# Attention on Trainium2: batches outside and head pairs inside, values of two pairs at once, a split output product

## The reference

```
def _L0_xattn_ref(x, context, w_q, w_k, w_v, w_o, b_o):   # 16 heads of 64, SCALE = 64 ** -0.5
    q = (x @ w_q).reshape(B, Sq, HEADS, DIM_HEAD).transpose(0, 2, 1, 3)
    k = (context @ w_k).reshape(B, Skv, HEADS, DIM_HEAD).transpose(0, 2, 1, 3)
    v = (context @ w_v).reshape(B, Skv, HEADS, DIM_HEAD).transpose(0, 2, 1, 3)
    sim = jnp.einsum('bhid,bhjd->bhij', q, k) * SCALE
    attn = jax.nn.softmax(sim, axis=-1)
    out = jnp.einsum('bhij,bhjd->bhid', attn, v)
    out = out.transpose(0, 2, 1, 3).reshape(B, Sq, INNER)
    return out @ w_o + b_o
...
x = x + _L0_xattn_ref(_layernorm(x, axis=-1), ctx_768, ...)
x = x + _L0_ffn_ref(_layernorm(x, axis=-1), ...)
x = x + _L1_xattn_ref(_layernorm(x, axis=-1), ctx_768, ...)
x = x + _L1_ffn_ref(_layernorm(x, axis=-1), ...)
```

## Time and profile before

| | |
|---|---|
| median of 3 runs | 2856.79 us (2854.0 to 2858.03) |
| the profiled execution: its time, its span | 2852.76 us, 2851.0 us |
| TensorE, VectorE | 2647.2 us (93%), 1999.4 us (70%) |
| ScalarE, GpSimd | 1290.9 us (45%), 1336.2 us (47%) |
| attention phases | some 38 to 993 us, and one as long in the second layer |

### The profile page before, as it was taken

One profiled execution on the slowest core, in us unless ns is written; L12 is line 12 of the kernel. 1 busy time (PEld: TensorE's weight loads), 2 busy tenths in 40 slices (PEclk: granted clock), 3 DMA queues, 4 the chain that ended last, 5 costly groups with the idle time before them and its releaser, 6 DMA issues. The chain is left out here.

```text
span 2851.0 us, 40294 instructions
## 1 busy us (share of the span) xinstructions
PE 2647.2 (93%) x13254; PEld 1814.1 (64%) x13254; DVE 1999.4 (70%) x2552; ACT 1290.9 (45%) x1891; POOL 1336.2 (47%) x1054
## 2 busy tenths in 40 slices
PE   3999999999999879999999689999999999996895
PEld 2556565656565468888888555656565656554785
DVE  5677677777676567777777657677777767764795
ACT  3545454545454333333333344545454545443394
POOL 4665656565656501111111145656666565652245
PEclk9999999999999989999999789999999999997997
DMA  3111111111111020000000010111111101103312
GB/s 109 39 30 33 30 29 33 37 26 35 35 24 33 16 67 22 24 26 22 22 28 17 10 39 23 41 29 33 29 36 27 40 22 38 27 23 116 121 50 86
DMA packets 48850, 108.85 MB, mean 38 GB/s; under 512 B 7200, under 2 KB 22432, under 8 KB 47776
## 3 DMA queue, kind: packets, MB, share of 16 engines
q1 hardware_dynamic: 43952, 101.01, 12.5%
q0 software_dynamic: 1536, 4.20, 0.5%
q10 hardware_dynamic: 3312, 3.02, 0.3%
HBM read 47.64 MB, written 10.22 MB: 20 GB/s over the span
## 5 line engine op out<-in xcount | busy, mean ns | idle before, releaser
L372 POOL TENSOR_TENSOR L1a_psums<-L1a_psums,L1a_probs 128x512 f32<-128x512 f32 x384 | 481.3, 1302 | 50.0 <-ACT L1a_probs L407 50.0
L372 POOL TENSOR_TENSOR L0a_psums<-L0a_psums,L0a_probs 128x512 f32<-128x512 f32 x384 | 481.1, 1297 | 49.7 <-ACT L0a_probs L407 49.7
L471 DVE TENSOR_REDUCE L1a_row_max<-psum 128x2 f32<-128x2048 f32 x128 | 293.5, 2293 | 150.9 <-PE psum L584 150.8
L471 DVE TENSOR_REDUCE L0a_row_max<-psum 128x2 f32<-128x2048 f32 x128 | 293.5, 2293 | 150.7 <-PE psum L584 150.7
L802 POOL TENSOR_TENSOR L0e_w_lo<-L0e_raw,L0e_w_hi 128x768 fp32r<-128x768 f32 x34 | 63.7, 1873 | 497.7 <-ACT L0e_w_hi L816 497.7
L407 ACT ACTIVATE L1a_probs<-psum 128x1024 f32<-128x1024 f32 x256 | 253.4, 1025 | 76.7 <-PE psum L611 75.2
L407 ACT ACTIVATE L0a_probs<-psum 128x1024 f32<-128x1024 f32 x256 | 253.3, 1025 | 73.8 <-PE psum L611 72.2
L624 PE MATMUL psum<-L0a_probs,L0a_v 128*64 128x512 f32 x1024 | 247.3, 605 | 0.0
L624 PE MATMUL psum<-L1a_probs,L1a_v 128*64 128x512 f32 x1024 | 247.3, 604 | 0.0
L856 DVE SCALAR_TENSOR_TENSOR xres<-psum,L0e_weights_of,xres 128x256 f32<-128x256 f32 x544 | 225.6, 477 | 22.7 <-PE psum L1029 21.8
L372 POOL TENSOR_TENSOR L1a_psums<-L1a_probs 128x512 f32<-128x512 f32 x64 | 81.4, 1294 | 322.1 <-ACT L1a_probs L407 322.1
(11 more groups left out here) (348 smaller groups left out, 6224.4 us busy)
## 6 DMA issues: line engine op xcount, KB each, us to landing
L0a_k_hs<-L0a_k_st SPq DMA_DIRECT2D x64, 256.0 KB, 3.5
L1a_k_hs<-L1a_k_st SPq DMA_DIRECT2D x64, 256.0 KB, 3.4
L0e_raw<-in_experts SPq DMA_DIRECT2D x34, 384.0 KB, 3.0
L1weights<-in_sorted SPq DMA_DIRECT2D x2, 6144.0 KB, 17.9
L0a_q_hh<-L0a_q_hh SPq DMA_DIRECT2D x64, 128.0 KB, 2.3
L1a_q_hh<-L1a_q_hh SPq DMA_DIRECT2D x64, 128.0 KB, 2.3
L0a_raw<-in_attention SPq DMA_DIRECT2D x8, 384.0 KB, 3.2
L1a_raw<-in_attention SPq DMA_DIRECT2D x8, 384.0 KB, 3.1
```

The costliest lines, as they stand in the source:

```text
L372: nc.gpsimd.tensor_tensor(psums[:, h, :], a, probs[:, h, kv, :], ALU.add).then_inc(sem["acc"], 1)
L471: nc.vector.reduce_max(row_max[:, qt, 0:2 * 32].rearrange("p (h n) -> p h n", h=2)[:, :, 0], psum[:, 0:4 * BANK].rearrange("p (h k) -> p h ...
```

## The change

- Batches are the outer loop and head pairs the inner one. The context is loaded and split one batch ahead, in the first segment of each batch (`prepares`), and the first normalisation does only batch 0.
- Each segment has its own weights: loaded and split in each segment, into two alternating halves of `w_split`. ScalarE takes the high part, GpSimd (before: VectorE) the remainder. The output weights are part of them.
- Values are projected for two pairs at once, five products of 256 columns for each 128 keys, in one block ahead of the rounds in each even segment. One ScalarE copy replaces a copy and an addition.
- The rounds are two value products, then scores.
- The output is split: a copy on ScalarE (`high_output`), a subtraction on VectorE (`low_output`), and three fast products for each slow one.
- The high part of the queries is taken by VectorE (`high_queries`), the copies of keys on ScalarE follow the first exponentials, and VectorE's reciprocal stands ahead of K0's remainder. The bias is added by VectorE.

```
-WCOL = (KD + 4) * P
+WCOL = (KD + 2) * P + DIM
+VCOL = 4 * P
...
                     def run(eng, segment):
-                        segment(0, 0, first=True)
-                        with eng.Fori(0, HP - 1) as hp:
-                            for b in range(1, BATCH + 1):
-                                segment(hp, b)
-                        for b in range(1, BATCH):
-                            segment(HP - 1, b, ahead=b < BATCH - 1)
+                        for b in range(BATCH):
+                            segment((0, HP * b), b, first=b == 0)
+                            with eng.Fori(0, HP // 2 - 1) as r:
+                                segment((r, HP * b + 1), b)
+                                segment((r, HP * b + 2), b)
+                            segment((0, HP * b + HP - 1), b, ahead=b < BATCH - 1)
...
+                        def low_weights(s):
+                            par = s[1] % 2
+                            pool.wait_ge(sem["whi"], count(s, 1, 1))
+                            nc.gpsimd.tensor_tensor(w_split[:, par, 1, :], raw[:, :], w_split[:, par, 0, :], ALU.subtract)\
+                                .then_inc(sem["wlo"], 1)
...
+                        def high_output(s):
+                            act.wait_ge(sem["norm"], count(s, 1, 1))
+                            nc.scalar.activation(o_split[:, 0, :], o_sb[:, :], ACT.Copy).then_inc(sem["ohi"], 1)
+
+                        def segment(s, b, first=False, ahead=True):
+                            max_rows(s)
+                            exps(s, 0)
+                            exps(s, 1)
+                            if ahead:
+                                high_keys("K0", after(s))
+                            exps(s, 2)
+                            if ahead:
+                                high_keys("K1", after(s))
+                            exps(s, 3)
+                            exps(s, 4)
+                            if not first:
+                                high_output(before(s))
...
+                        def high_queries(s):
+                            par, src = s[1] % 2, bank(PLACE["Q"])
+                            dve.wait_ge(sem["proj"], count(s, 3, 3))
+                            for h in range(2):
+                                nc.vector.tensor_copy(q_hh[HEAD[h], par, h, :], src[HEAD[h], :]).then_inc(sem["qhi"], 1)
...
+                        def low_output(s):
+                            dve.wait_ge(sem["ohi"], count(s, 1, 1))
+                            nc.vector.tensor_tensor(o_split[:, 1, :], o_sb[:, :], o_split[:, 0, :], ALU.subtract).then_inc(sem["olo"], 1)
...
-                        def project_values(piece, hp, b, added=True):
-                            batch, n = b % BATCH, VALUES.index(piece)
...
-                                nc.tensor.matmul(both, ctx_hi[:, keys_of], w_split[:, :, WV[0]], start=True, stop=False)
-                                nc.tensor.matmul(both, ctx_hl[:, keys_of], w_split[:, :, WV[1]], start=False, stop=False)
-                                last = nc.tensor.matmul(both[:, 0, :], ctx_lo[:, keys_of], w_hi[:, WV[0]], start=False, stop=True)
...
+                                last = split_product(bank(PLACE[piece])[:, i * 2 * P:(i + 1) * 2 * P],
+                                                     [(hi, wv[:, 0, WV[0]]), (hi, wv[:, 1, WV[0]]), (lo, wv[:, 0, WV[0]]),
+                                                      (hl, wv[:, 0, WV[1]]), (hl, wv[:, 1, WV[1]])])
...
-                                pe.wait_ge(sem["norm"], count(hp, 1, b, 1))
-                                pe.wait_ge(sem["wo"], (hp + b // BATCH) * 16 + 16)
+                                pe.wait_ge(sem["olo"], count(s, 1, 1))
...
-                                last = nc.tensor.matmul(bank(PLACE[f"OUT{half}"])[:, n * DIM:(n + 1) * DIM],
-                                                        o_sb[:, t * P:(t + 1) * P], wo_sb[:, :], start=True, stop=True)
+                                last = split_product(bank(PLACE[f"OUT{half}"])[:, n * DIM:(n + 1) * DIM],
+                                                     [(o_hi[:, rows], w_hi), (o_hi[:, rows], w_lo), (o_lo[:, rows], w_hi)])
...
+                            if even(s):
+                                for piece in VALUES:
+                                    project_values(piece, s, b, first)
                             for qt in range(QT):
-                                pv(hp, b, 2 * qt, first)
-                                pv(hp, b, 2 * qt + 1, first)
+                                pv(s, 2 * qt, first)
+                                pv(s, 2 * qt + 1, first)
                                 if ahead:
-                                    score(hp, b + 1, qt)
-                                    project_values(VALUES[qt], hp, b + 1, not first)
+                                    score(after(s), qt)
```

More of the change, by code:

```diff
@@ new lines, in segment @@
+                            for p in range(5, 8):
+                                exps(s, p)
+                            if even(s):
+                                for piece in VALUES:
+                                    values(piece, s)
+                            if s[1] != LAST[1]:
+                                if not first:
+                                    act.wait_ge(sem["out"], count(before(s), 2, 2))
+                                high_weights((s[0], s[1] + 3))
+                                if even(s):
+                                    high_values((s[0], s[1] + 2))
@@ L486, in add_output, with segment @@
                                 rows = xres[:, t:t + 2, :].rearrange("p t d -> p (t d)")
-                                dve.wait_ge(sem["out"], count(hp, 2, b, half + 1))
-                                dve.wait_ge(sem["added"], count(hp, 2, b, half + 3))
+                                dve.wait_ge(sem["out"], count(s, 2, half + 1))
+                                dve.wait_ge(sem["added"], count(before(s), 2, BEFORE + half + 1))
                                 nc.vector.tensor_tensor(rows, bank(PLACE[f"OUT{half}"]), rows, ALU.add).then_inc(sem["added"], 1)
-                        def segment(hp, b, first=False, ahead=True):
-                            split = b == BATCH - 2 and not isinstance(hp, int)
+                        def segment(s, b, first=False, ahead=True):
+                            if not first:
+                                invert(before(s))
@@ L526, in _ @@
+                        normalise(LAST)
+                        low_output(LAST)
+                        add_output(LAST, BATCH - 1)
                     @block.tensor
@@ L651, in output, with segment @@
                             last.then_inc(sem["out"], 1)
-                        def segment(hp, b, first=False, ahead=True):
+                        def segment(s, b, first=False, ahead=True):
+                            nb = (s[1] + 1) // HP if isinstance(s[0], int) else b
                             if ahead:
-                                keys("K0", hp, b + 1)
-                            transpose_max(hp, b, first)
+                                keys("K0", after(s), nb)
+                            transpose_max(s)
@@ L673, in segment @@
-                            qk(hp, b, 6)
-                            qk(hp, b, 7)
+                                output(before(s), 0, ahead)
+                            qk(s, 6)
+                            if not first and even(s):
+                                output(before(s), 1, ahead)
+                            qk(s, 7)
+                            if not first and not even(s):
+                                output(before(s), 1, ahead)
+                            if even(s):
+                                for piece in VALUES:
+                                    project_values(piece, s, b, first)
```

515 lines of the change are left out of this document (267 added, 248 removed).

## The result

The changed kernel takes 3270.9 us (median of 4, 3266.2 to 3274.6), beside 2855.4 for the kernel before in the same rounds: a ratio of 1.145, with an interval of 1.143 to 1.147. The direction and nearly all steps of the forecast of 3170 us came true; some 100 us came on top, and they have one cause.

The account below looks back on a forecast made before the run. TensorE, busy 93%, was taken to bound the kernel, VectorE's reduction close behind. Rounds −0.5, value block +2.4 and output wait +3.4 made +5.3 us a segment, +316 with the ends, so 3170 us (range 3090 to 3270).

Parts of the forecast that it names:

- The clock falls: Rival, 11%: TensorE's 2.9 us standstill per segment halves its clock for what follows; at most 205 us, 3375 us.
- in one segment of three: Milder case of the rival "The clock falls": the clock drops in only a third of segments, giving 3240 us.
- twelve at half the clock: Last segment of a phase: eight slow output products, 3.78 us, shrink to twelve at half clock, some 2.6 us.
- The rounds lose their cover: Attention rounds: without value projection, VectorE's reduction chain sets 3.19 us per round; four gain 0.5 us per segment.
- The value block: Ahead of even segments' rounds: 40 products of 256 columns take 4.8 us per two segments, +2.4 us per segment.
- The output now waits: Part one of each segment: output waits some 2.9 us for VectorE's `low_output`; part one grows by 3.4 us.
- Sum: Attention segments: odd 31.6, even 36.4, mean 34.0 us against 28.73; with phase ends and first normalisation, +316 us.
- At no cost: Weight splits and loads in each segment, next batch's context split and VectorE's bias: covered by idle time, adding nothing.
- The first normalisation: Three quarters of the context split leaves the first normalisation, whose GpSimd work had stretched VectorE: −7 us.
- Only the rounds count: Rival, 8%: `low_output` ends by T + 10.8 (T: the transposes), so only +1.9 us per segment stays; some 2970 us.
- faster: Rival, 4%: VectorE keeps pace and TensorE sets the time, 27.3 us per segment, −90 us, 2765 us.
- the 0.3 for outputs and 0.6 for values: TensorE's savings per segment: six fast output products for two slow ones 0.3 us; values 3.0 to 2.4, 0.6 us.

Follow-up runs that it names:

- e1: Changed kernel plus eleven extra 512-column products per segment on TensorE, filling the wait ahead of the output, result overwritten: 3157.5 us, ratio 1.106.
- e6: e2 plus the value projection of two pairs spread over eight rounds of two segments, one tile in each: 2884.5 us, ratio 1.010.
- e2: Changed kernel with `low_output` ahead of the query copies and query remainder, and ScalarE's output copy ahead of the fourth exponential: 2987.3 us, ratio 1.047.
- e7: e6 plus K0's copy ahead of the maxima on ScalarE and its remainder ahead of the reciprocal on VectorE: 2827.8 us, ratio 0.991.
- e9: e1 with the high query copies back on ScalarE, ahead of its fifth exponential: 3164.2 us, ratio 1.106.

## Why the prediction was wrong

The step that failed is the one that left the clock out of the sum. "The clock falls" stood among the rivals, with 11% and with "in one segment of three" as its milder case, on the reading that across the wait of 4.19 us near the phase's end TensorE "kept the upper level longer". The clock falls in nearly every segment, so its price belonged into the sum. I had priced it (3240 for a third of the segments, 3375 at most); the time lies between the two and just above my range, which took in only the milder case.

The reading was wrong. The same wait of the kernel before in shorter stretches:

```profile
984.50:988.70 4.20, 0.01 (x2) 0.00 (x1) 4.05 (x2) 0.00 (x0) 0.00 (x0) 0.65 0.00 0
988.70:992.00 3.30, 3.30 (x8) 2.50 (x8) 0.69 (x1) 0.00 (x0) 0.00 (x0) 0.50 0.00 0
```

The clock fell inside the wait, and the outputs behind it ran wholly at the lower level, as in the changed kernel's even segments. The 0.84 was a mean over 22 us, with the busy time ahead of the wait in it. The forecast held a sign of this: its own sum says "twelve at half the clock" of the outputs behind that very wait, which took 0.47 us each, where the loop's take 0.22 (four in 0.87).

What the fall costs is measured by e1: 113 us, 1.8 for each of 62 segments. The segments shown agree: 38.73 and 32.99 less e1's 36.30 and 31.48 are 2.4 and 1.5 us. The trace of before has this wait a second time, at the end of the second layer's phase (4.19 us at 2583.26), and the clock fell there too.

The other steps, each by its own number:
- **The rounds lose their cover.** A round is 3.12 us (517.51 to 520.63, and so on), forecast 3.19. Right, with its 0.52 us of idle time released by L531.
- **The value block.** 507.64 to 512.51 is 4.87 us, forecast 4.8. Right; e6 gives the sum of both steps from the other side.
- **The output now waits.** Idle 2.70 us, forecast 2.9; e2 takes out the whole of it, 170 us. `low_output` 1.17, forecast 1.3; the queries' wait 0.61, forecast 0.8. This was the largest term, and right.
- **Sum.** 3170 against 3158 with the clock held. Right within its bounds. One slip is in it: the terms of part one as given, 12.45 + 1.3 + 3.3 + 1.87, are 18.9 and not 18.8, which makes some 5 us over the 60 periods.
- **At no cost.** GpSimd's splits of weights (1.83 and 1.27 us at 514.03 and 515.82) end in its idle time, and nobody waits for them. Right.
- **The first normalisation** ends its last remainder at 30.3 instead of 38.0 us: 8, forecast 7. The operation of 16 columns that had taken 2.25 us takes 0.17.
- **Rivals.** "Only the rounds count" and "faster" fell by the order of VectorE, as argued: e2 is the former made true, 2987 against 2970 forecast for it.

From after to e7 the runs account for the change: 113 us of clock, 170 of the output's wait, 103 of values without cover, 57 of K0's late remainder. What is left in e7, 0.51 us a segment under the kernel before (26 us by its ratio), is about half of the 0.3 for outputs and 0.6 for values that the forecast had counted as TensorE's savings. The outputs' 0.3 is there (two halves of 0.71, before 0.87 each). The values' 0.6 is not: alone in its round a tile takes 0.78 us (538.12 to 538.90), where the block's count has 0.6, the first two products 0.34 instead of 0.24 and a gap behind the last. Four tiles are 3.1 us, before 3.3.

## What to carry to other kernels

When a change leaves TensorE idle once per period, as here for 2.7 us, and the trace of before has even one stretch that shows a fall of the clock around such a wait, put the fall into the sum and not among the rivals: here 1.8 us on top of the 2.7. Order VectorE's queue by who is waited for: one subtraction (and the copy that feeds it) moved ahead of the query operations was worth 170 us, and 284 with the clock that came back. Work that hides a fixed chain (here 3.1 us of score, reduction and hand-over) is not saved by being gathered elsewhere: spread it so that each round of the chain has just enough.

## What the hardware showed that I had not expected

- **The clock** went to its lower level in each of the six segments read, at one idle time of 2.7 us, and stayed there 3.4 us in the odd and 6.8 us in the even ones, though TensorE worked without a pause once the output had started; at 1.8 us it fell in four of six, for 3.4 us each. Waits of 0.5, 0.6 and 1.0 us (e2) left the granted clock at 1.00 over 400 us. The kernel before shows one fall around a wait of 1.54 us (2555.12, in the second layer's last segments), and none around the like one of 1.55 us in the first (962.13). Why equal waits bring a fall or none, and falls of different lengths, wasn't settled.
- **The price of one subtraction with both inputs in SBUF** went from 0.69 to 1.71 us with what GpSimd did when it started: 0.72 in the mean in e2, 1.17 after, 1.66 in e9 (1.71 in the row shown). The Trainium skill (SBUF — State Buffer, section "SBUF: two separate sides") has the later of the two wait; the rows agree: 0.69 us in e2 with GpSimd idle at its start, more where GpSimd was adding. Moving an operation changes its price as well as its place.
